# Shared passes of equal width behind four groups of attention, with low-rank features in four column tiles

## The reference, cut to what matters

```python
x = x + attention(layernorm(x), ctx, ctx, itok)   # 8 batches, 8 heads of 32 rows, 512 positions
x = x + moe(layernorm(x))

def moe(xt):                                      # 2048 tokens of 512 features
    top_p, top_i = top_k(softmax(xt @ gate_w), 2) # 8 experts, at most 320 tokens each and choice
    out = sum over k of kept[e] * top_p[k] * (
        gelu(xt @ w1[e] + b1[e]) @ w2[e] + b2[e] + gelu(xt @ wd[e]) @ wu[e])
    sh = gelu(xt @ sw1 + sb1) @ sw2 + sb2         # the shared expert: 512 -> 2048 -> 512
    sh = sh + gelu(xt @ swd) @ swu                # its low-rank side: 512 -> 32 -> 512
    return out + 0.2 * sh
```

## Time and profile before

| | us |
|---|---|
| median of the runs | 1333.91 |
| the profiled execution | 1338.04 |
| its span, first to last instruction | 1336.2 |
| TensorE busy | 1293.7 (97%) |
| VectorE busy | 841.5 (63%) |
| ScalarE busy | 708.5 (53%) |
| GpSimd busy | 253.1 (19%) |
| mean granted TensorE clock | 0.987 of full speed |

### The profile page before, as it was taken

One profiled execution on the slowest core, in us unless ns is written; L12 is line 12 of the kernel. 1 busy time (PEld: TensorE's weight loads), 2 busy tenths in 40 slices (PEclk: granted clock), 3 DMA queues, 4 the chain that ended last, 5 costly groups with the idle time before them and its releaser, 6 DMA issues.

```text
span 1336.2 us, 26800 instructions
## 1 busy us (share of the span) xinstructions
PE 1293.7 (97%) x10963; PEld 943.0 (71%) x11024; DVE 841.5 (63%) x1420; ACT 708.5 (53%) x1056; POOL 253.1 (19%) x219
## 2 busy tenths in 40 slices
PE   6788999999999999999999999999999999999997
PEld 2152736465554646384888889999999988888895
DVE  7777779797888887763742835638266383562730
ACT  5867676758676776662533524535244353442521
POOL 4740010000000051514200302203022030120112
PEclk7899999999999999999999999999999999999999
DMA  9614141423284332416736757677586775867313
GB/s 283 217 33 126 48 119 41 119 56 99 68 79 98 80 80 88 120 33 127 216 106 142 197 140 213 143 157 197 135 210 140 138 203 139 196 153 137 96 25 40
DMA packets 195627, 168.21 MB, mean 126 GB/s; under 512 B 117945, under 2 KB 138569, under 8 KB 195506
## 3 DMA queue, kind: packets, MB, share of 16 engines
q1 hardware_dynamic: 183218, 141.30, 40.7%
q0 software_dynamic: 12288, 25.21, 11.1%
HBM read 109.47 MB, written 34.15 MB: 107 GB/s over the span
## 4 chain that ended last, share of the span: by engine, by line
PE 88%; ACT 4%; issue 2%; DVE 2%; DMA 2%; SPq 1%; POOLq 0%; POOL 0%; another core or an unknown queue 0%; ACTq 0%; DVEq 0%
PE banks L1920 25%; PE banks L1950 24%; PE banks L1854 12%; PE banks L1836 10%; PE banks L1776 5%; PE banks L1756 4%; PE banks L1724 3%; ACT QS L1137 1%; DMA split_parts<-hidden 1%; PE banks L1810 1%; PE banks L1785 1%; ACT hf L1196 1%; ACT hidden L1150 1%; PE banks L1961 1%; PE banks L1822 1%
## 5 line engine op out<-in xcount | busy, mean ns | idle before, releaser
L1950 PE MATMUL banks<-hidden,w2h 128*128 128x0 bf16 x2048 | 306.1, 269 | 0.0
L1150 ACT ACTIVATE hidden<-banks,scales 128x512 f32<-128x512 f32 x256 | 170.4, 688 | 86.4 <-PE banks L1756 55.3
L1950 PEld LDWEIGHTS banks<-hidden,w2h 128*128 128x128 bf16 x2048 | 198.6, 98 | 20.5
L1378 DVE TENSOR_REDUCE rowmax<-banks 128x1 f32<-128x512 f32 x256 | 172.8, 686 | 33.0 <-PE banks L1724 31.6
L1950 PE MATMUL banks<-hidden,w2l 128*128 128x0 bf16 x1024 | 192.3, 269 | 0.0
L1529 DVE TENSOR_TENSOR w1l<-stage,w1h 128x2048 bf16<-128x2048 f32 x32 | 73.2, 2292 | 187.7 <-ACT w1h L1227 187.7
L1854 PE MATMUL banks<-w2h,hidden 128*128 128x512 bf16 x498 | 179.1, 379 | 0.8 <-issue 0.5
L1244 ACT ACTIVATE hf<-banks,b1cols 128x640 f32<-128x640 f32 x128 | 101.4, 793 | 122.4 <-PE banks L1920 108.8
L1255 ACT ACTIVATE yT<-banks 128x640 uint16<-128x640 uint16 x56 | 36.4, 702 | 215.2 <-PE banks L1950 215.2
L1920 PE MATMUL banks<-eth,w1h 128*128 128x0 bf16 x1024 | 133.0, 273 | 0.0
L1920 PE MATMUL banks<-etl,w1h 128*128 128x0 bf16 x1024 | 132.9, 273 | 0.0
(11 more groups left out here) (199 smaller groups left out, 1966.4 us busy)
## 6 DMA issues: line engine op xcount, KB each, us to landing
stage<-in_L_ffn_w SPq DMA_DIRECT2D x64, 1024.0 KB
split_parts<-hidden SPq DMA_DIRECT2D x16, 512.0 KB, 4.9
QS<-split_parts SPq DMA_DIRECT2D x48, 128.0 KB, 2.7
KS<-split_parts SPq DMA_DIRECT2D x48, 128.0 KB, 3.2
xin<-in_x SPq DMA_DIRECT2D x16, 256.0 KB, 3.8
cin<-in_ctx SPq DMA_DIRECT2D x16, 256.0 KB, 3.9
out_rows<-xin SPq DMA_DIRECT2D x16, 256.0 KB, 2.0
normed_rows<-x2r SPq DMA_DIRECT2D x16, 256.0 KB, 3.4
```

What stands on the lines that cost most here:

```text
L1150: ac.activation(prob[n % NPH], bank(score_bank[unit]), ACT.Exp, scale=scales[:, g // 2:g // 2 + 1]).then_inc(s_exp, 1)
L1378: dv.reduce_max(rowmax[g % 2][:, i:i + 1], bank(score_bank[unit]), X_AXIS).then_inc(s_max, 1)
L1950: issued = mm(bank(b0 + j)[:, skips[j]:CAP].shape_from_register(used_cols(e, j)), w[:, fb, rows], of_choice(a[:, fb, :], j, skips[j]).shap ...
```

## The change

There are eight passes of two groups each. Pass p holds groups 2p and 2p + 1, and it is run in the up pass of window p + 1, the last one alone; the downs of pass w - 2 stand beside the exponentials of window w. So the exponentials of groups 0 to 3 come first, with no shared work beside them, laid out by the new `ahead_of_passes`, which puts the layer norm, the operand split, the softmax's end and the tokens' transposition of neighbouring groups at fixed steps between them. Six score units of the group after next are issued ahead in the last six steps. Weight quarters are loaded and split two to a group; the last one is loaded and split in the first up pass. Group 2 leaves SUMMED. The low-rank features are computed by quarters of the 256 tokens in four tiles of 32 columns, in bank 3 for all passes but the first, and read by four activations; the split of their result (`low`) is issued after the fifth `up` unit of the pass.

```diff
-FIRST = [0, *range(1, GROUPS, PASS // P), GROUPS]
+FIRST = [*range(0, GROUPS + 1, PASS // P)]
...
-SUMMED = [2, *range(4, GROUPS)]
+SUMMED = [*range(4, GROUPS)]
...
-AHEAD = 10
+AHEAD = 6
...
-    p = (g + 1) // 2
+    p = g // 2
...
             add("up", p, fb)
+            if fb == 4:
+                add("low", p)
...
-        downs = [shared_down(w - 1, c) for c in range(len(groups_of(w - 1)))]
+        downs = [shared_down(w - 2, c) for c in range(len(groups_of(w - 2)))]
...
-        for n, _ in enumerate(shared_up(w)):
+        for n, _ in enumerate(shared_up(w - 1)):
...
-            if w == 0 and n in (2, 3):
-                add("turn_v", a + n)
...
+            if w == 1:
+                if n == 5:
+                    add("w_load", 7)
+                elif n == 9:
+                    add("w_split", 7)
+                elif n > 9:
+                    low_pieces()
...
+                for g in range(2, 4):
+                    add("c_load", g)
+                for n in range(2):
                     add("w_load", n)
...
+            if i == 13:
+                units(2, "stats", "aggr", "rstd")
...
+    def ahead_of_passes(g, score, side):
+        rows = max_rows(g + 1)
+        ahead = scores((g + 2) * UNITS, (g + 3) * UNITS)
         for i in range(UNITS):
+            add("exp", g, i)
             next(score, None)
+            if i >= UNITS - AHEAD and g < 2:
+                next(ahead)
+            if g < 3:
+                if i == 12:
+                    add("parts", g + 1)
+                if i == 14:
+                    next(rows)
+                if i > 13:
+                    next(rows, None)
+                    next(rows, None)
+            if g:
+                if i == 0:
+                    units(g + 2, "stats", "aggr", "rstd")
+                    if g > 1:
+                        units(g - 2, "xt_lo", "logit")
+                if i == 2:
+                    add("norm", g + 2)
+                if i == 3:
+                    units(g + 2, "x_hi", "x_lo")
+                if i == 4:
+                    units(g + 2, "c_lo", "bounce")
+                chain = {5: ("den",), 6: ("attn",), 7: ("resid",), 8: ("stats2",), 9: ("aggr2", "rstd2"),
+                         11: ("norm2",), 13: ("turn",), 15: ("gate",)}
+                for name in chain.get(i, ()):
+                    if name == "den":
+                        for k in range(3):
+                            add("den", g - 1, k)
+                    else:
+                        add(name, g - 1)
+                if i == 9 and g < 3:
+                    add("turn_v", g + 1)
+                if i == 11 and g < 3:
+                    add("load", g + 3)
+                    add("c_load", g + 3)
+            side(i)
+            if i < 4 and g:
+                half_step(g - 1, i + 10)
             if i > 5:
+                half_step(g, i - 6)
+        if g < 3:
+            for _ in rows:
+                pass
+        else:
+            units(g - 1, "xt_lo", "logit")
+        return ahead
+    def split_and_lows(i, n, first, then):
+        if i == first:
+            add("w_split", n)
+        if i == then:
+            add("w_split", n + 1)
+        if first < i < first + 5 or i > then:
+            low_pieces()
+    def beside_first(i):
+        split_and_lows(i, 0, 5, 11)
+        if i == 0:
+            add("norm", 2)
+        if i == 1:
+            units(2, "x_hi", "x_lo", "c_lo", "bounce")
+            for n in range(2, 4):
+                add("w_load", n)
+        if i == 7:
+            add("fills", 1)
+        if i == 9:
+            add("b2_parts")
+    def beside_second(i):
+        split_and_lows(i, 2, 5, 11)
+        if i == 5:
+            for n in range(4, 7):
+                add("w_load", n)
+        if i == 13:
+            add("wu", E)
+    def beside_third(i):
+        split_and_lows(i, 4, 6, 11)
+        if i == 10:
+            add("split_v", 4)
+        if i == 13:
+            add("wd", E)
+    early_scores = scores(4 * UNITS, 4 * UNITS + EARLY)
+    def beside_fourth(i):
+        if i == 12:
+            add("w_split", 6)
+        if i > 12:
+            low_pieces()
+        if i == 5:
+            add("join_v", 4)
+            add("split_v", 5)
+        if i >= UNITS - EARLY:
+            next(early_scores)
+        if i in (1, 14):
+            for _ in rows2(i // 14):
+                pass
     first_scores()
+    for _ in max_rows(0):
+        pass
+    score = scores(UNITS, 2 * UNITS)
+    for _ in range(AHEAD):
+        next(score)
+    for g, side in enumerate((beside_first, beside_second, beside_third, beside_fourth)):
+        score = ahead_of_passes(g, score, side)
+        if g > 1:
+            score = iter(())
+    low_pieces(1)
     first_part, early, placed, routing = [], [], [], []
-    for w in range(WINDOWS):
+    for w in range(1, WINDOWS):
...
-        hstage += [xt_stage[:, :], *(hidden[:, k * FB * PASS:(k + 1) * FB * PASS].bitcast(F32) for k in range(2)), late_stage[:, :]]
+        hstage += [*(hidden[:, k * FB * PASS:(k + 1) * FB * PASS].bitcast(F32) for k in range(2)), late_stage[:, :], late_stage[:, :]]
...
-                first = w == 0 or (unit[0] == "score" and g == 2 and i < AHEAD)
...
+                first = g < (4 if unit[0] == "score" else 3)
...
+        def rank_in_sums(p):
+            return p == PASSES - 1 or 2 * p + 3 in SUMMED
...
                 elif kind == "rank":
...
-                    ac.activation(lowf[:, 0:w], bank(b)[0:WIDE, 0:w], ACT.Gelu).then_inc(s_rgelu, 1)
+                    q = w // RANK_TILES
+                    for c in range(RANK_TILES):
+                        issued = ac.activation(lowf[0:RANK, c * q:(c + 1) * q], bank(b)[c * RANK:(c + 1) * RANK, 0:q], ACT.Gelu)
+                    issued.then_inc(s_rgelu, 1)
...
+                elif kind in ("low", "e_rank"):
...
+                    w = P * len(groups_of(m)) if kind == "low" else SLOTS
+                    link(dv.tensor_copy(o[0:RANK, 0:w], lowf[0:RANK, 0:w]))
+                    link(dv.tensor_copy(o[2 * RANK:3 * RANK, 0:w], lowf[0:RANK, 0:w]))
+                    dve.wait_ge(s_dve, chain)
+                    dv.tensor_tensor(o[RANK:2 * RANK, 0:w], lowf[0:RANK, 0:w], o[0:RANK, 0:w], ALU.subtract).then_inc(s_low, 1)
...
+                    if g % 2:
+                        pe.wait_ge(s_rgelu, g // 2)
...
+                    b = 3 if rank_in_sums(p) else shared_bank(unit)
+                    if p == PASSES - 1:
+                        pe.wait_ge(s_den, GROUPS)
...
-                            issued = mm(bank(b)[0:WIDE, 0:w], weights[:, kb, :], data[:, kb, 0:w], start=n == 1, stop=n == 3 * KB)
+                            for c in range(RANK_TILES):
+                                issued = mm(bank(b)[c * RANK:(c + 1) * RANK, 0:q], weights[:, kb, :],
+                                            data[:, kb, c * q:(c + 1) * q], start=n == 1, stop=n == 3 * KB)
```

171 lines of the change are left out of this document (39 added, 132 removed).

## The result

The changed kernel takes 1345.75 us (median of five runs, 1341.43 to 1345.94) against 1333.91 (median of five, 1332.96 to 1335.8): a ratio of 1.0076, 95% interval 1.0065 to 1.0087. Forecast were 1330.7 us and "faster"; it is slower, and outside the range of 1322 to 1340. The profiled executions differ by 7.7 us (1345.76 and 1338.04), and that is the sum to be explained.

What follows compares the result with a forecast made beforehand. PE's own work was taken to bound the kernel from 137.3 us on, except in the first stages and last pass. Merging -0.4, start -0.3, rank -1.0, last pass -1.5 sum to -3.2: median 1333.9 to 1330.7 us, range 1322 to 1340.

Steps and rivals of the forecast that it cites:

- I take 115.9, and the term is 115.9 - 116.2 = -0.3 us: First four groups: pass 0's rank starts at 115.9 us against a break-even of 116.2; bounds -7.6 and +10.3.
- The waits for operands: First four groups: PE waits for the operands' DRAM round trip, 2.9 us in group 0 and 4.4 in group 1.
- 2.0 of other loss: Groups 0 and 1: flat addition to ACT's summed work and the operand wait, giving 22.6 and 25.9 us.
- PE has about 2 us less: Group 3: less PE work than the similar earlier stage from 118.7 to 137.3 us, whose 18.6 us was taken.
- Rival 2: First four groups: operand waits and lower clock slow PE; 1339.6 us if group 3 ends behind 122; chance 0.25 with Rival 4.
- Nothing is late. DVE no longer waits at the head of a pass for the rank's result; PE has no idle time there to win back: Up passes: the new rank's four activations and DVE's changed waiting were given no cost or gain in PE time.
- The gain of the rank itself: All eight passes: ranks in four column tiles at 1.1 us each, 8.8 instead of 9.8 us, a term of -1.0.
- Rival 4: Windows: rank in bank 3 makes the ones step wait, 1 us in six windows, 1336.7 us; chance 0.25 with Rival 2.
- go by the trace: Rank: trace's 20 ns a matmul preferred to the skill's 25 ns floor, which would give about +1.4 instead of -1.0.
- -1.5 us: Last pass: two thirds of the stalls named issue may vanish and the counts' wait goes; bounds 0 and -3.9.
- the counts' wait: Last pass: the 0.4 us wait on the router's counts goes, since the routing chain's DVE steps have twice the time.
- the last weight quarter: First up pass: the moved quarter, 1.9 us on ACT, hides because ACT has room; without cover it would cost 1.9.

Runs made afterwards that it cites:

- a_again: The changed kernel, unaltered, timed again in a later session: median 1341.28 us, ratio 1.0036 to the kernel before.
- a_warm: a_low1 with each transposed score matmul of the exponentials of groups 0 to 3 issued twice: 1337.25 us, ratio 1.0010 to the kernel before.
- b_rank_low2: The kernel before with only the new low-rank side, its split behind the third up unit: 1340.69 us, ratio 1.0030 to the kernel before.
- a_low1: The changed kernel with the low-rank split behind the second up unit instead of the fifth: 1336.09 us, ratio 0.9997 to the kernel before.
- b_rank_low1: The kernel before with only the new low-rank side, its split behind the second up unit: 1334.17 us, ratio 0.9982 to the kernel before.

## Why the prediction was wrong, step by step

**The start.** The step that failed first is "I take 115.9, and the term is 115.9 - 116.2 = -0.3 us". In a_again it is +5.6, in the first profile +9.6, both inside the bounds given (-7.6 and +10.3) and not near the value taken. The waits for operands, on which the argument spent its care, came to 5.7 and 5.9 us instead of 7.3; what failed is the work and the loss beside them. By group, forecast and a_again: 22.6 and 23.05 (from 27.0), 25.9 and 28.3, 22.0 and 22.2, 18.6 and 21.2. So three things:
- *Group 1, +2.4.* The operands' wait was right here (4.4 forecast, 4.2 and 4.4 measured; group 0's was 1.6 and 1.3, not 2.9). The "2.0 of other loss" was not: PE waits there for 1.4 us on row maxima, 1.2 on MS, 0.9 on exponentials, 0.5 on issue, at a clock of 0.88.
- *Group 3, +2.6.* "PE has about 2 us less" than the stage of 18.6 us of before was wrong: it has 16.75 us, where that stage has 16.26, and waits of 4.9 us (4.0 of them on ACT), where that stage had 3.3.
- *The clock, +4.0 in the first profile* and 0 in a_again. Rival 2 had named it, as a price of every additional stage without shared work. Its test, "if group 3's exponentials end behind 122 us", came out at 124.8 in the first profile and at 120.8 in a_again, and its 1339.6 is nearer than the forecast. But of its mechanism only half holds. The granted clock is 0.86 to 0.90 in the four groups of the first profile, near its 0.83; but the operands came no later than forecast, and a_warm shows that keeping PE busy does not bring the rank forward.

The deeper fault was to sum one engine's work per group and to add a flat loss. With PE, DVE and ACT each busy for 70 to 80% of the stage, in one fixed order, every single relief of 12 us or more on ACT or DVE gave 0 to 4 us, and 12 us more on PE cost none of the rank's start. What exactly ties groups 1 and 3 is not settled by these runs: the reliefs show that maxima, exponentials, operands and the load of later rows follow close on one another, not which of them the unaltered order ends on.

**The rank.** "Nothing is late. DVE no longer waits at the head of a pass for the rank's result; PE has no idle time there to win back" is the other step that failed, and the experiments show it. The gain of the rank itself was undervalued: 0.49 us each instead of 1.1 us, -5.9 instead of -1.0 for eight; the windows confirm 0.7 each. The split was put down at nothing, though its three operations take 0.96 us of DVE (0.27 + 0.28 + 0.41), and they stand in a stretch in which DVE has next to no room (9.8 of 10 us busy in b_rank_low2, 9.4 in the changed kernel). That costs 5.6 us between the first rank and the last (456.70 and 451.13), and by the ratios of a_low1 and the changed kernel (0.9997 and 1.0036) 5.2, about what the new rank saves with its split in the better place (456.57 with the old one, 451.13). The prediction looked at who waits for the rank, not at what stands behind its split on DVE; the earlier trace rows gives DVE 365 of 455 us, an average in which this stretch cannot be seen. The trace of the kernel before does show it, in the window of a stretch that begins 9.3 us behind a rank:

```profile
290.00:300.00 10.00, 10.00 (x87) 8.25 (x85) 9.93 (x25) 5.87 (x14) 0.56 (x1) 1.00 0.07 26
```

DVE was already busy for 9.93 of 10 us there, PE for all ten. Rival 4 looked at this step for a wait at the ones step; none is in the trace.

Of the rule of the Trainium skill ("TensorE: Matmul & The Clock Gate", the section on 56 against 53.3 ns: about 25 ns between the starts of matmuls however narrow) the forecast said that it would go by the trace. The trace after has 10 ns a matmul in four column tiles, further below the rule than the 20 ns of the earlier trace rows.

**The last pass and the merging.** "-1.5 us" for the stalls, and the counts' wait gone: PE is busy for 21.96 of 22.01 us there, no stall is left. The four downs have 41.94 of 42.10. Both were right, and 2.0 us better than forecast.

**The first window** is the one the forecast missed: it takes 73.39 us where the four behind it take 71.97, and in the kernel before it was no longer than the others. Of these 1.4 us, 0.6 stand in b_rank too (72.52 and 71.94), which has the new rank without the new order, and 0.6 in a_rank_old (72.30 and 71.71), which has the new order without the new rank. The forecast put the last weight quarter, which is split in this window, at nothing because ACT has room; whether it is the quarter that costs the 0.6 is not settled.

**The sum** for the profiled pair: start +9.6 against even, windows +1.6, end -3.4 (17.7 less the 21.1 that moved), together +7.8 of the 7.7 measured. With the start of a_again it would be +3.8, and with the split behind the second `up`, 5.6 less, -1.8; that kernel, a_low1, measures 0.9997, -0.4 us. The difference of 1.4 is that of the profiled execution of before, 1338.04, which lies 1.5 above the 1336.6 of the same kernel beside a_low1.

## What to carry to other kernels

Before an operation is called free, look at the engine that carries it in the ten microseconds in which it will stand, in that engine's own timeline with its bracketed idle times; one gap of 1.4 us made the difference between -0.7 and +0.25 us a window, and the wrong side of one subtraction missed it. Where several engines hand each other short pieces in a fixed order and each is 70 to 80% busy, do not sum the busiest one and add a constant: take the length of a measured stage of the same make, count each engine's work for it again, and widen the range. And compare a start only between executions of one session whose matmuls run slow and fast in the same places: look at the matmul rows, for the printed clock can miss a stretch.

## What was not expected of the hardware

- 48 matmuls of 64 columns in four column tiles of 32 take 0.48 us, 10 ns each, where 12 over 256 columns took 1.31: 2.7 times less for the same features.
- Two executions of the same program differ by 4.0 us in the first four groups, and the times fall into two groups, 1341 and 1346. Matmul rows at the lower clock stand in both; those behind the operands' wait made the difference in group 0. The mean clock of an execution does not tell the two apart: of a_again's runs one of 1341.28 us has 0.987 and the one of 1346.24 has 0.991.
- When PE was given 12 us more to do in these groups, the granted clock printed for the whole stretch was 0.96 instead of 0.94: more work of this kind did not bring it to 1.00.
- Moving 13 us of copies from ACT to POOL went with operations of DVE up to about twice as long (538 to 1157 ns for the normalisation of the rows, a_act).
- A pitch can grow without a wait in the list: between 209 and 567 us b_rank_low2 has no wait for row maxima among those that are named for PE, and 0.98 us more in each window than b_rank_low1.
